# TensorE's two layers as a loop of seven rounds, with 401 chunks of edges, in a graph network kernel

## What is computed

```python
def _ngcf_conv(x, W1, W2, src, dst, n_nodes):
    deg_out = jnp.clip(jax.ops.segment_sum(ones, src, num_segments=n_nodes), 1.0)
    deg_in = jnp.clip(jax.ops.segment_sum(ones, dst, num_segments=n_nodes), 1.0)
    norm = jax.lax.rsqrt(deg_out[src] * deg_in[dst])
    h_src = x[src]
    h_dst = x[dst]
    msg = (h_src @ W1 + h_src * h_dst @ W2) * norm[:, None]
    agg = jax.ops.segment_sum(msg, dst, num_segments=n_nodes)
    return x @ W1 + agg

h = _ngcf_conv(x, W1_1, W2_1, edge_src, edge_dst, n)
h = jax.nn.relu(h)
h = _ngcf_conv(h, W1_2, W2_2, edge_src, edge_dst, n)
x = _layernorm(x + h, axis=-1)
```

## Time and profile before

| | us |
|---|---|
| timed runs (three) | 1152.91 median, 1151.71 to 1153.17 |
| profiled execution, span | 1700.1 |
| PE busy in the profiled execution | 1004.6 (59%) |
| DVE busy | 998.9 (59%) |
| POOL busy | 831.9 (49%) |
| ACT busy | 728.1 (43%) |
| gathers begin from table 0 / from table 1 | 140.7 / 946.3 |

### The profile page before, as it was taken

One profiled execution on the slowest core, in us unless ns is written; L12 is line 12 of the kernel. 1 busy time (PEld: TensorE's weight loads), 2 busy tenths in 40 slices (PEclk: granted clock), 3 DMA queues, 4 the chain that ended last, 5 costly groups with the idle time before them and its releaser, 6 DMA issues. The chain is left out here.

```text
span 1700.1 us, 33320 instructions
## 1 busy us (share of the span) xinstructions
PE 1004.6 (59%) x13036; PEld 885.6 (52%) x13036; DVE 998.9 (59%) x2383; ACT 728.1 (43%) x2707; POOL 831.9 (49%) x819
## 2 busy tenths in 40 slices
PE   2661565656555655665488256667666666666656
PEld 1641354546445544554478135556665555556556
DVE  8992663445534543454378335666667666766557
ACT  3001133435534534453478103555444445554446
POOL 5786435533554455345510555555555555554550
PEclk9996566676766766676779567776777767777778
DMA  9861111111111111111111312322433332233322
GB/s 212 207 242 22 19 23 38 46 34 41 47 37 44 35 46 37 42 37 43 37 48 54 75 30 53 66 60 58 82 64 64 65 66 66 53 65 64 65 63 56
DMA packets 148697, 106.56 MB, mean 63 GB/s; under 512 B 115832, under 2 KB 128568, under 8 KB 147900
## 3 DMA queue, kind: packets, MB, share of 16 engines
q1 hardware_dynamic: 122856, 71.17, 15.5%
q0 software_dynamic: 25472, 32.83, 10.5%
q10 hardware_dynamic: 212, 0.42, 0.1%
HBM read 59.25 MB, written 45.11 MB: 61 GB/s over the span
## 5 line engine op out<-in xcount | busy, mean ns | idle before, releaser
L799 POOL DMA_INDIRECT c_rows<-table,k_row_i x398 | 386.5, 971 | 405.7 <-PE c_sum L828 226.1
L799 POOL DMA_INDIRECT k_rows<-table,k_row_i x350 | 344.9, 985 | 388.6 <-DVE c_yr L1099 289.0
L828 PE MATMUL c_sum<-c_rows,c_sel 128*128 128x64 bf16 x4665 | 265.5, 223 | 263.7 <-issue 241.9
L828 PEld LDWEIGHTS c_sum<-c_rows,c_sel 128*128 128x128 bf16 x4665 | 232.1, 118 | 296.1 <-issue 295.4
L926 ACT ACTIVATE c_uvt<-c_turn 128x512 f32<-128x512 f32 x196 | 106.4, 596 | 649.5 <-PE c_turn L860 606.5
L1136 DVE TENSOR_TENSOR c_sum<-c_sum,c_own 128x512 f32<-128x512 f32 x94 | 65.6, 698 | 473.2 <-PE c_sum L828 426.7
L853 PE MATMUL c_out<-k_wcat,c_uvt 128*128 128x64 f32 x1504 | 218.6, 307 | 77.9 <-ACT c_uvt L926 57.6
L828 PE MATMUL c_sum<-c_lo,c_sel 128*128 128x64 bf16 x1555 | 219.6, 218 | 71.8 <-issue 71.7
L828 PE MATMUL c_sum<-c_yr,c_sel 128*128 128x64 bf16 x1555 | 220.9, 218 | 68.6 <-issue 67.9
L853 PEld LDWEIGHTS c_out<-k_wcat,c_uvt 128*128 128x128 f32 x1504 | 206.5, 219 | 101.1 <-ACT c_uvt L926 74.7
L828 PE MATMUL c_sum<-c_rest,c_sel 128*128 128x64 bf16 x1555 | 220.1, 218 | 64.1 <-issue 64.0
(11 more groups left out here) (210 smaller groups left out, 1247.8 us busy)
## 6 DMA issues: line engine op xcount, KB each, us to landing
table<-c_y SPq DMA_DIRECT2D x48, 384.0 KB, 2.3
out<-c_y SPq DMA_DIRECT2D x48, 256.0 KB
c_res<-in_x SPq DMA_DIRECT2D x46, 256.0 KB
c_rows<-table,k_row_i POOLq DMA_INDIRECT x398
k_rows<-table,k_row_i POOLq DMA_INDIRECT x350
table<-k_xh SPq DMA_DIRECT2D x1, 3640.0 KB
table<-k_xh SPq DMA_DIRECT2D x2, 1820.0 KB
table<-k_xh SPq DMA_DIRECT2D x1, 3542.5 KB
```

Of the source, the lines that this page charges most:

```text
L799: nc.gpsimd.indirect_dma_start(out=rows[:, b % RING, i], out_offset=None, in_=tables[l], in_offset=bass.IndirectOffsetOnAxis(ap=k.row_i[:, ...
L828: last = nc.tensor.matmul(p_sum[g % BANKS][:, t - GROUP[g][0], :], sel[:, b % 2, i, n * P:(n + 1) * P], part[:, i], start=first and q == 0 ...
```

## The change

Nothing of what is computed changes. Five things do:

- The tiles' spacing becomes 49 chunks for 48 tiles, 130.67 places a tile (`BASES`), so that the pattern of chunks and tiles repeats exactly every 49 chunks. There are 401 chunks.
- `BATCH` becomes six batches of 8, seven rounds of 9, 8, 8, 8, 8, 8, and 4, 3, 3. A batch has `SLOTS` = 9 places in every buffer, and the rings shrink from (8, 4) to (7, 3) batches.
- TensorE's steps 6 to 47 become a loop (`Fori`) over seven rounds of six steps. Its waits inside the loop compare with a value made from the round's number in a register. The other engines' programs stay written out.
- The counts go over units of 8 chunks (`UNITS`), no longer over batches, and lie in steps 5 and, of each round, 0, 2, 4 in layer one (22), and 0 to 3 of each round and step 4 in layer two (29; the last unit is one chunk). TensorE's `tally` follows the loop.
- The scan's input is made by two instructions, as 130.67 times the tile's number has to be rounded.

```diff
-CAP = 130
+ROUND_TILES, ROUND_CHUNKS = 48, 49
+CAP = ROUND_CHUNKS * P / ROUND_TILES
-CHUNKS = 398
+CHUNKS = 401
+def base_of(t):
+    return (2 * ROUND_CHUNKS * P * t + ROUND_TILES) // (2 * ROUND_TILES)
+BASES = [base_of(t) for t in range(TILES)]
 def band(c):
-    return range(max(0, (P * c - REACH) // CAP + 1), min(TILES - 1, (P * c + P - 1) // CAP) + 1)
+    return [t for t in range(TILES) if BASES[t] <= P * c + P - 1 and BASES[t] + REACH > P * c]
...
-            step(V.scalar_tensor_tensor(ahead, tile_i, float(CAP), kb, ALU.mult, ALU.subtract))
+            step(V.tensor_scalar(ahead, tile_i, float(CAP), WHOLE, ALU.mult, ALU.add))
+            step(V.scalar_tensor_tensor(ahead, ahead, -WHOLE, kb, ALU.add, ALU.subtract))
...
-BATCH = [8] * 49 + [4, 2]
+STEPS_A_ROUND = 6
+ROUNDS = 7
+BATCH = [8] * STEPS_A_ROUND + [9, 8, 8, 8, 8, 8] * ROUNDS + [4, 3, 3]
+SLOTS = max(BATCH)
-RINGS = (8, 4)
+RINGS = (7, 3)
...
-COUNT_AT = [{s: (s - 8) // 2 for s in range(8, 45, 2)}, {}]
-COUNT_AT[1] = {s: len(COUNT_AT[0]) + i for i, s in enumerate(s for s in range(42) if s % 4 != 3)}
+UNITS = [(c, min(c + 8, CHUNKS)) for c in range(0, CHUNKS, 8)]
+COUNT_STEPS = [(5, (0, 2, 4)), (4, (0, 1, 2, 3))]
...
+            def until(semaphore, first, turn, more):
+                pe.wait_ge(semaphore, first if turn is None else turn * more + first)
-            def add_up(b):
-                pe.wait_ge(sel_made, b + 1)
-                pe.wait_ge(split, b + 1)
+            def add_up(b, turn=None):
+                until(sel_made, b + 1, turn, STEPS_A_ROUND)
+                until(split, b + 1, turn, STEPS_A_ROUND)
...
-            for s in STEPS:
+            def one_step(s, turn=None):
                 if s in LOOKUPS:
...
+            for s in range(STEPS_A_ROUND):
+                one_step(s)
+            with pe.Fori(0, ROUNDS) as turn:
+                for s in range(STEPS_A_ROUND, 2 * STEPS_A_ROUND):
+                    one_step(s, turn)
+            if l == 1:
+                tally()
             add_up(b0)
```

More of the change, by code:

```diff
@@ L610 @@
 assert max(COUNT_AT[1]) < VERDICT
[L611 removed]
+assert sorted(COUNTS[0] + COUNTS[1]) == list(range(len(UNITS)))
 assert FIRST[-1] == CHUNKS
@@ L627, in ended @@
     return [g for g in range(GROUPS) if ENDS[g] == s]
+for s in range(STEPS_A_ROUND, STEPS_A_ROUND * ROUNDS):
+    again = s + STEPS_A_ROUND
+    assert BATCH[again] == BATCH[s] and FIRST[again] == FIRST[s] + ROUND_CHUNKS
+    assert ended(again) == [g + STEPS_A_ROUND for g in ended(s)] and len(ended(s)) == 1
+    for c in range(FIRST[s], FIRST[s + 1]):
+        assert band(c + ROUND_CHUNKS) == [t + ROUND_TILES for t in band(c)]
+        assert [g + STEPS_A_ROUND for g in range(GROUPS) if BEGINS[g] == c] == [g for g in range(GROUPS) if BEGINS[g] == c + ROUND_CHUNKS]
+assert STEPS_A_ROUND % BANKS == STEPS_A_ROUND % RINGS[1] == STEPS_A_ROUND % 2 == 0
 def layer(nc, l, x, out, tables, flag, keepers):
@@ L833, in add_up, with count, multiply @@
                         meet(LOOKUPS[b], 5 + i)
-            def count(b):
-                pe.wait_ge(hots_made, COUNTS[l].index(b) + 1)
-                for i in range(BATCH[b]):
-                    last = nc.tensor.matmul(k.p_count[:, 0:TILES], hot_l[:, :, i], hot_t[:, i], start=l == 0 and b == COUNTS[0][0] and i == 0,
-                                            stop=l == 1 and b == COUNTS[1][-1] and i == BATCH[b] - 1, skip_group_check=True)
+            def count(u, turn=None):
+                a, b = UNITS[u]
+                until(hots_made, COUNTS[l].index(u) + 1, turn, len(COUNT_STEPS[l][1]))
+                for i in range(b - a):
+                    last = nc.tensor.matmul(k.p_count[:, 0:TILES], hot_l[:, :, i], hot_t[:, i], start=u == COUNTS[0][0] and i == 0,
+                                            stop=True, skip_group_check=True)
                 last.then_inc(counted, 1)
-            def multiply(g):
-                pe.wait_ge(uvt_made, g + 1)
+            def multiply(g, turn=None):
+                until(uvt_made, g + 1, turn, STEPS_A_ROUND)
                 if g in (g2, g3):
                     pe.wait_ge(uv_made, GROUPS)
-                else:
-                    done(pe, y_made if l == 0 else centred, g - 1)
+                elif g >= 2:
+                    until(y_made if l == 0 else centred, g - 1, turn, STEPS_A_ROUND)
                 weights = k.wcat[:, l, :]
@@ L876, in tensor @@
                 for g in ended(s - 2):
-                    multiply(g)
-                add_up(s)
+                    multiply(g, turn)
+                add_up(s, turn)
                 for g in ended(s - 1):
-                    turn(g)
+                    turn_over(g, turn)
                 if s in COUNT_AT[l]:
-                    count(COUNT_AT[l][s])
-                if l == 1 and s == VERDICT + 1:
-                    tally()
+                    count(COUNT_AT[l][s], turn)
+            if l == 0:
+                pe.wait_ge(k.lead_done, 1)
+                pe.wait_ge(k.w_in, 64)
+            for b in LOOKUPS.values():
+                turn_lanes(b)
+            for s in range(STEPS_A_ROUND):
[5 more added lines that the diff above has]
+                tally()
             add_up(b0)
             multiply(g0 - 1)
-            turn(g0)
+            turn_over(g0)
             add_up(b1)
@@ L1066, in norm_of @@
                 step(V.tensor_tensor(q, q, d, ALU.mult))
-                step(V.scalar_tensor_tensor(rows[:, b, :, D], q, 1.5, r, ALU.add, ALU.mult))
+                step(V.scalar_tensor_tensor(rows[:, b, 0:8, D], q, 1.5, r, ALU.add, ALU.mult))
             def select(b):
```

52 lines of the change are left out of this document (26 added, 26 removed).

## The result

The kernel after takes **1171.52 us** (median of 4 runs, 1169.9 to 1175.99) where the kernel before takes 1152.31 (4 runs): a ratio of 1.0146, interval 1.0117 to 1.0174, so slower by 1.5%, or 19.2 us. The forecast was 1174.6 in 1152 to 1198.

A forecast was written before the change was run, and what follows sets the result against it. GpSimd's gathers were taken to bound the kernel, with a base of 1139 us plus small waits up to the measured 1152.9. The change's terms added 21.7 us, giving 1174.6 us, range 1152 to 1198.

The forecast's parts named there:

- Chunks: GpSimd, both layers: 401 chunks instead of 398 issue 6 more gathers at 1.25 us on the path, +7.5 us.
- Ring of seven: Layer one: batch 12 waits for the sixth cut, one batch sooner than before, +5 us (0 to about +11).
- Scan in two passes: VectorE before the scan: one more pass over 98x1024, +1.2 us, or nothing if early gathers absorb it.
- Ends: End of each layer: last batches 4, 3, 3 leave VectorE's chain ending after the gathers, +3 us a layer, +6.
- Ring of three and late counts: Layer two: ring costs 0, but counts in steps 42 to 45 leave VectorE's lag, +2 us (0 to +10).
- The loop: TensorE: 12 backward branches cost 4 to 48 us of its time, but 0 on the path.
- Counts: VectorE: three more units counted in layer one, three fewer in layer two; worth 0 while GpSimd leads.
- One, branches felt: TensorE has no room for 12 branch stops of up to 4.0 us each: about 1210 us, chance 0.11.
- Two, VectorE: VectorE bounds layer two, which then doesn't pay for its gathers and gains three counts: 1162 us, chance 0.13.
- Three, code supply: TensorE waits for code blocks, 0.37 us each; repeated rounds save 28 us: about 1141 us, chance 0.12.
- Four, rings cost nothing: Rings and tails cost nothing, only gathers count: +7.5 to +9, 1161 us; within the forecast's chance of 0.64.
- What would show it: Profile after: 353 and 401 gathers, median 945 ns, GpSimd blocked once more; a far larger span fall means recording holes.

The follow-up runs named there:

- the run meant to settle it: Kernel before with 395 chunks a layer and last batches 5, 3, 3, beside 395 chunks with 8, 4, 2: 1719.9 us, ratio 0.9986, in condition B.
- runs with double: Kernel after with a loop of three rounds of twelve steps, the seventh round of six written out: 1171.0 us, ratio 1.0178.
- half the loop: Kernel after with its loop kept in layer one and written out in layer two: 1168.1 us, ratio 1.0124.

## Why the prediction was right

The sum was made for a kernel whose gathers set the time, and that is what it is: 22 added gathers cost 28.6 us. The base was right for a reason that the runs don't bear out, and there was luck in that. I put the holes of the earlier trace rows down to the recording; they belong to condition B, and recorded runs in condition A don't have them. Leaving them out was right, since the times were of condition A. With layer one's and two's gathers at 1.314 and 1.274, as in the record after, the base is 140.7 + 350 x 1.314 + 18.6 + 398 x 1.274 + 20.6 = 1146.9, and before's median less the 1.6 around the span is 1150.7: some 4 us are left, not 14, and most of what I called small waits are, if before is like after in this, longer gathers of layer one.

One reading of TensorE was off. The eight turns of 1.83 us that open are not at the higher clock: the clock granted from 1165.9 to 1167 us is 0.50. At the higher level eight turns take 1.04 us (a row below), so TensorE needs 3.4 + 1.04 + 1.49 + 2.00 = 7.9 us a step and not 8.7. It made room for the loop, and changed no term. Now by the prediction's terms:

1. *Chunks*, +7.5. Six at 1.30 are 7.8. Right.

2. *Ring of seven*, +5. **Nothing**, by the record after. The failed step is the spacing of the first cuts. They were put at 135, 149.5, 164, 178.5, 193 and 207.5, by the earlier trace rows of condition B. The sixth came here, by VectorE's timeline, before the gather that it releases, batch 12's first:

```profile
201.79 0.69 DVE L1139 TENSOR_TENSOR c_yr<-k_rows 128x512 f32<-128x512 f32 x1
```

```profile
202.48 0.94 POOL L826 DMA_INDIRECT k_rows<-table,k_row_i  x1 [0.30 <-issue]
203.73 1.02 POOL L826 DMA_INDIRECT k_rows<-table,k_row_i  x1 [0.30 <-issue]
```

The first cut began at 135.9, as forecast, the next five 13.2 us apart and not 14.5. The slot was free at 202.48 and wanted at 203.73, so the margin is 1.25 us; with a ring of eight, batch 12 would have had one step more. It was a close call on the other side of the line, and the prediction had named it: at 13.5 us a step, nothing.

3. *Scan in two passes*, +1.2. The first table gather begins at 141.70 instead of 140.7: 1.0. The first of the early gathers, too, begins 1.0 later (49.06 instead of 48.07), so they absorb nothing. Right.

4. *Ends*, +3 a layer. VectorE's timeline of layer two, from the last full batch's split to the last split:

```profile
1127.34 0.72 DVE L1127 TENSOR_TENSOR c_rows<-c_rows 128x512 bf16<-128x512 f32 x1 [0.50 <-DMA c_rows<-table,k_row_i]
...
1134.29 0.45 DVE L1127 TENSOR_TENSOR c_rows<-c_rows 128x256 bf16<-128x256 f32 x1
...
1140.51 0.35 DVE L1127 TENSOR_TENSOR c_rows<-c_rows 128x192 bf16<-128x192 f32 x1
...
1143.57 0.36 DVE L1127 TENSOR_TENSOR c_rows<-c_rows 128x192 bf16<-128x192 f32 x1
```

1143.57 - 1127.34 is 16.2 us, as the prediction had it (16.6 before), and the last batch had landed at 1137.70 + 1.6 = 1139.3, so VectorE was **4.3 us** late. In layer one the last cut begins at 609.38, and its rows had landed at 605.62 + 1.6 = 607.2:

```profile
609.38 0.36 DVE L1139 TENSOR_TENSOR c_yr<-k_rows 128x192 f32<-128x192 f32 x1
```

2.2 us. Together 6.5 for the 6 forecast, of which a part is luck. The prediction took the landing of 1.6 us off the 3.7; but the batch from which the 16.2 us run lands 1.6 us after its gathers too, so the 3.7 stand, and with the third chunk they are 4.2. Layer two is this figure, layer one about half. That before loses nothing there is argued from the earlier trace rows; no record of it in condition A was to be had, and the run meant to settle it met B.

5. *Ring of three and late counts*, +2. The ring costs nothing: GpSimd has no wait on sums. Of the counts no lag was left, since the split of batch 47 waited 0.50 us for its rows (first row above).

6. *The loop*, 0: right, by the runs with double and half the loop, and by 12 branches of 0.2 us. 7. *Counts*, 0: it fits the gathers that never wait; no run changes the counts by themselves.

Together 7.8 + 1.0 + 6.5 = **15.3 us**, against 19.2, 15.5, 13.7 and 18.9 measured for the kernel after, the same again, and the two kernels that differ from it in the form of the loop alone. The forecast of 21.7 holds 7 us for rings and counts that cost nothing; that it lies within 2.5 us of 19.2 even so is in part luck. The four agree within their intervals. The largest piece of scatter that the traces show is **TensorE's clock in the last 20 us**, which the prediction didn't have. From the last split to the end it took 1168.3 - 1143.57 = 24.7 us in the kernel after and 1163.1 - 1144.10 = 19.0 in the kernel with half the loop. The stretch 1144 to 1156 us as a window (busy us of PE, PEld, DVE, ACT, POOL; granted clock; DMA), the first of the kernel after:

```profile
1144.00:1156.00 12.00, 10.75 (x79) 10.38 (x80) 8.45 (x19) 4.08 (x14) 0.00 (x0) 0.55 0.13 30
```

```profile
1144.00:1156.00 12.00, 8.70 (x97) 8.12 (x97) 10.92 (x26) 6.76 (x19) 0.00 (x0) 1.00 0.20 45
```

The same multiplication of 16, in the same order:

```profile
1151.36 3.68 PE L885 MATMUL c_out<-c_w_centred,c_uvt 128*128 128x64 f32 x16 [1.18 <-ACT c_uvt L966]
1154.83 1.91 PE L893 MATMUL c_turn<-k_ident,c_uv 128*128 128x128 f32 x8
```

```profile
1149.61 2.00 PE L885 MATMUL c_out<-c_w_centred,c_uvt 128*128 128x64 f32 x16 [1.18 <-ACT c_uvt L970]
1151.45 1.04 PE L893 MATMUL c_turn<-k_ident,c_uv 128*128 128x128 f32 x8
```

3.68 us near the lower level (1.2 GHz; 0.55 over the 12 us), 2.00 at the higher (2.4 GHz), and here TensorE is on the path. Between 1138 and 1144, just ahead, it was busy 2.23 of 6 us in the first and 3.70 in the second. Of six records of this family two had the short end (25.0 and 25.4 us after the last gather) and four the long one (30.6 to 31.8). That is a draw of 5 to 6 us from run to run, which would make a good part of the scatter from 1160 to 1176. A second piece is layer one's 353 gathers: their busy time in these records lies between 356.2 and 360.0 us.

The kernel before may have the same draw. Its seven runs on the second chip stand in two groups, three from 1145.5 to 1147.7 and four from 1152.1 to 1153.7 us. With the short end its base is the 1146.9 above, with the long one 1152.6, and 1150.7 was measured: it can't be said which. So the 3.9 us between 15.3 and 19.2 may be this clock, if before ended short, or the gathers' scatter, if it didn't, and no run here decides it. Whether the change alters the odds isn't known either.

The rivals. *One, branches felt*: out; 0.2 us where the code stays and about 4 where it doesn't, neither on the path. *Two, VectorE*: out for the kernel after, by ten gathers that cost 14 us; for the kernel before by the sum of its gathers only. *Three, code supply*: out in condition A, since 32, 68 and 112 packets give 1171.5 or 1167.6, 1168.1 and 1171.0; condition B looks like it, only twelve times as large as the rival had it (4.5 us a block, not 0.37). *Four, rings cost nothing*: right on the rings, and short by the ends. *What would show it*: the counts and the median (944 ns) of the gathers came as said. GpSimd wasn't blocked once more, as the ring's term had wanted. The fall of the profiled span, my sign for the recording, came with condition A in a record after. That sign didn't tell two causes apart.

## What to carry to other kernels

When the profile of a kernel and its timed runs differ by more than a few per cent, look first whether both are of one chip and one condition, and whether the two traces hold as many events, and put no cause to it before; here an engine's own work (instruction by duration, and the gap to the next) gave a good sum where every wait in the profile misled. Padding that makes rounds alike is paid in full on the engine that sets the time, 1.3 us for each added gather, and it shrinks the last batches, behind which another engine's chain comes out. Keep a loop's body on TensorE below the length that stays on the chip, which was between 1,540 and 3,100 instructions here.

## What the runs showed of the hardware

- A loop body of some 1,540 TensorE instructions is fetched once (32 packets in all), one of 3,100 on each turn (112 packets, against 103 unrolled); a backward branch instruction took 0.21 to 0.24 us in the one and 3.5 to 4.6 in the other.
- The same kernel takes 1152 us on two chips and 1722 on a third, all runs recorded, always to within a per cent. On the third TensorE loses some 4.5 us at each newly fetched block of 256 instructions, looped or not; on the others nothing, at up to 112 packets. The traces of the third hold less than half as many semaphore events. Why is open.
- A gather of 128 rows costs GpSimd 1.24 to 1.36 us with its gap, whether it brings 4 or 96 floats a row.
- The last 20 us of a kernel ran at either level of TensorE's clock, 19.0 or 24.7 us from the last split to the end, with the same program of that stretch.
